# Taking a group's 48 columns of x from a second on-chip copy instead of a transfer, in a two-layer graph network

## The reference

```python
tmp = concat([x[dst], x[src], edge_attr_32], axis=1)      # 48 + 48 + 32 = 128 columns
msg = relu(tmp @ W1 + b1) @ W2 + b2
x = layernorm(x + segment_sum(msg, dst))
m = relu(x[src] + edge_attr_48)
x = layernorm(x + (1 + eps) * x + segment_sum(m, dst))
```

## Time and profile before

| | |
|---|---|
| median of 3 runs | 4706.2 us (4700.16 to 4718.2) |
| profiled execution | 4705.52 us, span 4703.7 us |
| TensorE matmul busy | 4008.3 us, 85% of the span |
| VectorE busy | 1592.0 us, 34% |
| ScalarE busy | 791.9 us, 17% |
| GpSimd busy | 2679.7 us, 57% |
| granted TensorE clock, mean | 0.754 of full speed |
| first transpose of layer 0 | 35.4 us |
| last transpose of layer 0 starts at | 2443.5 us |

### The profile page before, as it was taken

How to read it: one execution, slowest core, us unless ns; L and a number is a source line. 1 busy time by engine, 2 the same in 40 slices (tenths; PEclk the granted TensorE clock), 3 DMA queues, 4 the chain that set the end, 5 groups by cost and what they waited for, 6 DMA issues and landing times.

```text
span 4703.7 us, 51904 instructions
## 1 busy us (share of the span) xinstructions
PE 4008.3 (85%) x19093; PEld 2794.8 (59%) x19093; DVE 1592.0 (34%) x3440; ACT 791.9 (17%) x1962; POOL 2679.7 (57%) x2838
## 2 busy tenths in 40 slices
PE   6888888888888888899998888888888888888988
PEld 3555555555555555565566666666666666666776
DVE  1111111111111111121125555555555555555565
ACT  1222222222222222222220000000000000001111
POOL 5666666666666666656545555555555555555554
PEclk7666666666666666666568888888888888888888
DMA  4111111111111111112111111111111111111111
GB/s 72 28 29 30 29 29 30 29 29 28 30 28 30 29 28 29 28 32 35 30 30 32 32 31 34 33 32 32 31 32 33 33 32 31 33 31 33 38 35 35
DMA packets 353293, 151.19 MB, mean 32 GB/s; under 512 B 278948, under 2 KB 352632, under 8 KB 352888
## 3 DMA queue, kind: packets, MB, share of 16 engines
q0 software_dynamic: 90688, 69.83, 10.0%
q1 hardware_dynamic: 260232, 75.09, 7.3%
q10 hardware_dynamic: 2114, 2.88, 0.4%
HBM read 142.76 MB, written 4.80 MB: 31 GB/s over the span
## 4 chain that ended last, share of the span: by engine, by line
PE 65%; another core or an unknown queue 14%; issue 11%; ACT 5%; DVE 4%; DMA 0%; DVEq 0%; SPq 0%
PE ps_h L681 17%; PE ps_h L645 12%; PE ps_t L681 9%; PE ps_sums L618 8%; PE ps_m L627 8%; PE ps_t L638 5%; PE ps_a L641 3%; ACT hT L528 2%; ACT edgeT L520 2%; PE ps_nodes L691 2%; DVE picked L864 2%; DVE at_place L856 1%; PE ps_t L673 1%; ACT w_edge L526 1%
## 5 line engine op out<-in xcount | busy, mean ns | idle before, releaser
L421 POOL DMA_INDIRECT edge<-x,resid_sb x1564 | 1478.9, 946 | 948.9 <-issue 471.4
L421 POOL DMA_INDIRECT edge<-x_dram,resid_sb x1270 | 1200.6, 945 | 1047.0 <-DVE pre L882 606.9
L681 PE MATMUL ps_h<-x_parts,at_place 125*128 125x480 f32 x3920 | 1037.8, 415 | 51.4 <-issue 49.1
L618 PEld LDWEIGHTS ps_sums<-edge,msg 128*48 128x48 f32 x6256 | 448.4, 154 | 872.7 <-issue 804.2
L681 PEld LDWEIGHTS ps_h<-x_parts,at_place 125*128 125x128 f32 x3920 | 785.1, 207 | 195.6 <-issue 79.7
L645 PE MATMUL ps_h<-edgeT,w_edge 128*128 128x512 f32 x782 | 692.5, 983 | 171.3 <-ACT w_edge L526 161.4
L618 PE MATMUL ps_sums<-edge,msg 128*48 128x48 f32 x6256 | 569.5, 245 | 222.1 <-issue 197.3
L823 DVE TENSOR_TENSOR acc<-acc,ps_sums 48x48 f32 x782 | 154.5, 198 | 1777.3 <-remote 1054.6
L681 PE MATMUL ps_t<-x_parts,at_place 125*128 125x480 f32 x1960 | 586.3, 434 | 129.5 <-issue 125.1
L627 PEld LDWEIGHTS ps_m<-w_sb,hT 128*128 128x128 f32 x3128 | 547.2, 263 | 118.2 <-issue 102.4
L627 PE MATMUL ps_m<-w_sb,hT 128*128 128x48 f32 x3128 | 603.8, 353 | 7.1 <-ACT hT L528 7.1
(11 more groups left out here) (65 smaller groups left out, 1590.1 us busy)
## 6 DMA issues: line engine op xcount, KB each, us to landing
e_sb<-e SPq DMA_DIRECT2D x196, 192.0 KB
edge<-e SPq DMA_DIRECT2D x196, 128.0 KB
edge<-x,resid_sb POOLq DMA_INDIRECT x1564
edge<-x_dram,resid_sb POOLq DMA_INDIRECT x1270
x_win<-xT SPq DMA_DIRECT2D x391, 9.0 KB
acc<-xT ACTq DMA_DIRECT2D x1, 2343.8 KB, 22.6
x_dram<-feats SPq DMA_DIRECT2D x10, 234.4 KB
out<-resid_sb SPq DMA_DIRECT2D x10, 234.4 KB
```

The lines of the kernel that those rows point to most:

```text
L421: pool.indirect_dma_start(out=cols, out_offset=None, in_=rows_of, in_offset=bass.IndirectOffsetOnAxis(ap=index, axis=0)).then_inc(done, 16)
L618: last = nc.tensor.matmul(sums, lhsT=msg[:, v, t, :], rhs=edge[:, v, t, 0:WIN], start=(t == 0), stop=(t == TILES - 1))
L681: last = nc.tensor.matmul(ps_picked[m], lhsT=at_place[:, m, c, :], rhs=x1_parts[:, c, part, :], start=(c == 0 and part == 0), stop=(c == C ...
```

## The change

A second copy of transposed x is loaded at the start into partitions 64 to 111 of `acc`, by a second transfer of ScalarE behind the first, and stays there. From iteration 4 on (`FIRST`), VectorE copies a group's 48 columns from it into `x_win`, ahead of the one-hot matrix of the same group, and SyncE issues no transfer for it; TensorE no longer waits for a window, since its wait for the one-hot matrix comes later in VectorE's order. The first 16 groups are loaded as before. VectorE needs the window's first node in a register one group earlier than before, so that `first_nodes` keeps what it loaded in a dictionary, for the copy and for `accumulate` together. The registers of layer 1 are held apart from those of layer 0.

```diff
+        kept_x = acc[P // 2:P // 2 + D, 0:N]
...
         def first_nodes(eng, held, name, i):
-            fresh = [eng.alloc_register(f"{name}{i}_{u}") for u in range(UNROLL)]
-            eng.load(fresh, base_row[0:1, i * UNROLL:(i + 1) * UNROLL])
-            values = [eng.snap(r, donate=True).with_bounds(min_val=0, max_val=N - WIN) for r in fresh]
-            for r in held:
-                eng.free_register(r)
-            held[:] = fresh
-            return values
+            if i not in held:
+                for old in [k for k in held if k < i - 1]:
+                    for r in held.pop(old)[0]:
+                        eng.free_register(r)
+                registers = [eng.alloc_register(f"{name}{i}_{u}") for u in range(UNROLL)]
+                eng.load(registers, base_row[0:1, i * UNROLL:(i + 1) * UNROLL])
+                held[i] = registers, [eng.snap(r, donate=True).with_bounds(min_val=0, max_val=N - WIN) for r in registers]
+            return held[i][1]
...
             def loads0(i, c):
-                starts = first_nodes(sp, held, "first", i)
                 for u in groups_of(i):
                     if u % 2 == 0:
                         wait_group(sp, S0["trans"], i, u + 1, back=UNROLL)
                         load_e32(S0["edges"][u // 2], i * 2 + u // 2, u)
-                    else:
+                    if i < FIRST:
                         wait_group(sp, S0["awin"], i, u, back=UNROLL)
-                    sp.dma_start(x_win[:, u, :], xT[:, bass.ds(starts[u], WIN)]).then_inc(S0["window"][u], 16)
+                        first = first_nodes(sp, held, "first", i)[u]
+                        sp.dma_start(x_win[:, u, :], xT[:, bass.ds(first, WIN)]).then_inc(S0["window"][u], 16)
...
             act.dma_start(acc[0:D, 0:N], xT).then_inc(s_xT, 16)
+            act.dma_start(kept_x, xT).then_inc(s_kept, 16)
             act.wait_ge(s_const, 16 * N_CONST)
...
-                    pe.wait_ge(S0["window"][u], i * 16 + 16)
+                    if i < FIRST:
+                        pe.wait_ge(S0["window"][u], i * 16 + 16)
...
+            def copy_window(i, u):
+                j, v = i + (u + 1) // UNROLL, (u + 1) % UNROLL
+                if j >= FIRST:
+                    if (j, v) == (FIRST, 0):
+                        dve.wait_ge(s_kept, 16)
+                    first = first_nodes(dve, held0, "first", j)[v]
+                    nc.vector.tensor_copy(x_win[:, v, :], kept_x[:, bass.ds(first, WIN)])
...
                     if not last_group(i, u):
+                        copy_window(i, u)
                         onehots(S0, i, u, iota_sb[:, :])
```

More of the change, by code:

```diff
@@ L202, in build @@
         s_xT = sem("s_xT")
+        s_kept = sem("s_kept")
         s_x = sem("s_x")
@@ L342, in _ @@
             sp.dma_start(src_all[:, first:], src_tiles[:, first:]).then_inc(s_src, 16)
-            held = []
+            held = {}
             def loads0(i, c):
-                starts = first_nodes(sp, held, "first", i)
                 for u in groups_of(i):
@@ L812, in onehots @@
                                         .to_broadcast([P, TILES, WIN]), ALU.is_equal).then_inc(S["onehot"], 1)
-            starts, held = [], []
+            held0, held1 = {}, {}
+            def copy_window(i, u):
[5 more added lines that the diff above has]
+                    nc.vector.tensor_copy(x_win[:, v, :], kept_x[:, bass.ds(first, WIN)])
             def accumulate(S, i, u, back):
-                if (u - back) % UNROLL == 0:
-                    starts[:] = first_nodes(dve, held, S["acc"].name, i + (u - back) // UNROLL)
-                first = starts[(u - back) % UNROLL]
+                first = first_nodes(dve, *((held1, "second") if S is S1 else (held0, "first")), i + (u - back) // UNROLL)[(u - back) % UNROLL]
                 if S is S1:
```

## The result

Median 4722.3 us (20 runs, 4706.42 to 4747.87) against 4708.2 us (20 runs): ratio 1.0034, 95% interval 1.002 to 1.0049, so 14 to 16 us slower (9 to 23 by the interval). 4724 was forecast. The profiled execution of the changed kernel took 4715.92 us, its span is 4714.1 us.

What follows compares the result with a forecast made beforehand. TensorE was taken to set layer 0 at 6.15 us per group, its start delayed by loading x. The second load's +18 us, all else 0, gave 4723.5 us (4724 by the median); range 4716 to 4733, widened to 4702 to 4736.

Steps and rivals of the forecast that it cites:

- The second load at the start: Start: 2.4 MB queued ahead of the first edge features moves TensorE's first transpose from 35.4 to about 53.4 us, +18 us.
- The rival that the load hardly holds up the start: Start: edge features get turns between rows of x, costing nothing to one row, 5.8 us, so 4709 us; chance 0.12.
- The window's transfer removed: Layer 0: 375 transfers, 3.5 MB, go; DMA is 19% busy and nobody waited for them, 0 us.
- The copy: VectorE, layer 0: 0.15 us per copy, 107 us in all with registers, hidden by 2.2 us idle per group, 0.
- The copy beside GpSimd: Layer 0: copies hold GpSimd's port, at worst 0.15 us per group, 56 us, within its 1.15 us free: 0.
- TensorE's wait removed: Weight load of L641, layer 0: its late start comes from its size, not the wait, 0; up to 100 us gained if wrong.
- The pace of layer 0: Layer 0: TensorE's five steps run without a gap and set 6.15 us per group, unchanged by the change.
- The sum: Whole kernel: 4705.5 us profiled plus 18 gives 4723.5 us, or 4724 us by the median.

Runs made afterwards that it cites:

- two repeats: Changed kernel timed again beside the kernel before: 4688.5 us, ratio 1.0004; and with its second load meant as 2000-byte rows, which were merged again: 4692.9 us, ratio 1.0001.

## Why the prediction was right or wrong

**The second load at the start: right.** +18 was the term, by three rows of 50,000 bytes per engine; the first transposes moved by 19.6 us. The load alone gave 15 us (1 to 29) in the whole time, and 21 at an equal clock. Cutting the first load of x, which was there before, brought the first transposes forward by 11 to 13 us, by the same mechanism from the other side.

**The rival that the load hardly holds up the start: wrong, and why.** The rule of the Trainium skill (DMA: Bandwidth & Descriptors, Queues, rings and completion order), turns between queues at each packet, agrees with the trace in that q1 did get a turn for each of q10's, 64 for 64. The 2 packets of the earlier trace rows, from which I took it that q1 hardly gets any, were not typical of what follows. The turns don't help, since one of q1's is worth a single packet of 128 bytes here, and one of the other queue a row of 50,000, some 5.8 us.

**The window's transfer removed, 0: right for the pace in the middle, not borne out in the whole time.** On the slow chip, with neither transfer nor copy, the time fell by 24 us (13 to 34) where the step says 0. I had looked only at who waited for these transfers. That they cost something as neighbours I took as excluded by 19% of busy DMA. Most of the 24 us goes with the clock: the kernels without the transfers were granted 0.764 to 0.766 on the slow chip and those with them 0.760, and at an equal clock the estimate leaves 5 ± 8 us. Why the clock was higher isn't settled. In the traces of the slow chip the gain lies late in the run. The last 90 groups of layer 0 take 560 to 567 us in the four traces without the transfers and 576 and 577 us in the two with them. Layer 1 (from ScalarE's last copy of a transposed group to the end) takes 2242 to 2249 us without and 2256 and 2260 us with them, although it has none of them in any kernel. These are single executions, and the runs of one kernel spread by 30 us and more. The same doesn't show on the quick chip.

**The copy, 0: right.** 192 ns in place of 150, the idle ahead of `b2` still 2 us per group, and nine further copies cost so little that the runs hardly tell it from nothing.

**The copy beside GpSimd, 0: right in size, incomplete in mechanism.** The average of GpSimd's instruction on the slow chip (300 to 1500 us) went from 944 to 948 ns, a little longer as I had said. But the copy of 48 × 48 is not what lengthens them: those that began beside one took 0.94 to 0.96 us, so I had carried the long COPY of the earlier trace rows over to one that is too short. I had not seen that the one-hot matrix lengthens them, and that the copy takes it out of the way. Where GpSimd sets the pace, this is a gain of 10 us by the traces and of 2 to 7 by the times at an equal clock.

**TensorE's wait removed, 0: right.** The idle ahead of the load of L641 is 101.8 us in 391 in place of 103.9. Carrying a wait was not the cause.

**The pace of layer 0: right for that chip alone.** I took TensorE as what sets it. On the quick chip the same program's layer 0 takes 5.0 us per group, and GpSimd has no idle time but the 0.30 us between instructions. I had worked out GpSimd's 5.0 us and used it only as a reserve.

**The sum.** +18 and 0 gave 4724 us, and 4722.3 was measured. That the whole time came out so near is partly luck. In the two repeats on a slow chip the ratios were 1.0004 and 1.0001, with the same late start; their intervals and that of the first comparison meet only at 1.002 to 1.0025. The late start is certain (54.5 to 55.2 us in every trace that has the second load at the front). What made up for it in the repeats goes with the higher clock: at an equal one the estimate is +16 and +22 us. The prediction had no term for a change of the clock.

## What to carry to other kernels

Before a large transfer goes to the front, look at what its rows are: few long rows hold each engine for microseconds, and short packets of other queues get at best one turn per row. Send what the first step needs, cut the rest into pieces and issue them behind the first iterations. And ask of a part that only "has reserve" by how much, since on another chip or at another clock it can be the one that sets the pace. Last, before a difference of half a per cent is put to a part of the kernel, compare the granted clocks of the runs.

## What the runs showed of the hardware

- The same program took 4687 to 4708 us in some sets of runs and 3725 to 3729 in others. The mean granted clock was 0.754 to 0.764 and 0.856 to 0.868, which alone is less than the difference; on the slow chip much of VectorE's idle time in layer 0 is put to an unknown releaser (`remote` in the rows above, 440.0 us ahead of L835), and on the quick one none from 300 to 1500 us.
- VectorE's one-hot matrix, a comparison of two tiles in SBUF, lengthens an indirect transfer of GpSimd that starts with it or up to 0.2 us later: 0.96 to 1.2 us in place of 0.94. The Trainium skill (SBUF — State Buffer, SBUF: two separate sides) has a rule that VectorE with two SBUF inputs contends with an operation of GpSimd that reads SBUF; these traces agree that the two contend. They don't agree that the one that starts first keeps the other out to its end: in the kernel before on the quick chip, 147 of 258 one-hot matrices ran inside an instruction of GpSimd, in their usual 0.34 us.
- From 29.2 to 47 us of the changed kernel the turns between two queues on the same engines went packet for packet, whatever their size: 64 of SyncE's 128-byte packets against 64 packets of ScalarE's queue, 48 of them rows of 50,000 bytes.
- Copies of 48 × 48 one behind the other follow at 0.1 us, though each takes 0.18 to 0.2 us.
